# One block for the four stages behind the attention, with the loads of each inside the one in front

## The reference, cut to what matters

```python
x = x + tanh(g_xattn[0]) * cross_attention_16_heads(layernorm(x), ctx, mask)
x = x + tanh(g_ffn[0]) * expert_choice(layernorm(x))
#     softmax over 8 experts; each expert takes its 512 best tokens (top_k of the scores),
#     mid = silu(tokens @ W_up[group] + b_up); out = mid @ W_down[e] + b_down
#     y.at[idx].add(score * out): a token can be taken by several experts
x = x + tanh(g_xattn[1]) * bidirectional(layernorm(x), ctx)
#     Sim = e@w1 + q@w2 + (e*w3)@q.T + b;  hq = softmax(Sim) @ q;  hc = softmax(max(Sim)) @ e
#     concat[e, hq, e*hq, e*hc] @ W_qv + b_qv
x = x + tanh(g_ffn[1]) * first_choice(layernorm(x))
#     each token goes to its argmax expert while that has room for 512; gate * (x @ W[e].T + b[e])
```

## Time and profile before

| | |
|---|---|
| median of 3 runs | 819.12 us (817.71 to 821.33) |
| the profiled execution | 816.21 us |
| its span, first to last instruction | 814.5 us |
| PE / DVE / ACT / POOL busy | 654.6 / 435.8 / 317.2 / 276.8 us |
| mean granted TensorE clock | 0.907 of full speed |
| bytes moved | 99.96 MB, 123 GB/s |

### The profile page before, as it was taken

How to read it: one execution, slowest core, us unless ns; L and a number is a source line. 1 busy time by engine, 2 the same in 40 slices (tenths; PEclk the granted TensorE clock), 3 DMA queues, 4 the chain that set the end, 5 groups by cost and what they waited for, 6 DMA issues and landing times. The chain is left out here.

```text
span 814.5 us, 14651 instructions
## 1 busy us (share of the span) xinstructions
PE 654.6 (80%) x5225; PEld 452.9 (56%) x5225; DVE 435.8 (54%) x1306; ACT 317.2 (39%) x677; POOL 276.8 (34%) x386
## 2 busy tenths in 40 slices
PE   5999988999999850128999999953799999980783
PEld 3666545555555530023666666642688888860672
DVE  5646556777777637752111111102568887761683
ACT  2333335777777742223222222202655555310220
POOL 4101102344433411023555553332224444324275
PEclk9999999999999985557999999995899999996797
DMA  8579933666665119134363643227434341112772
GB/s 269 192 168 266 246 105 71 132 127 124 127 123 126 47 62 216 2 95 128 68 146 55 159 90 63 26 27 242 128 104 131 130 131 53 54 52 86 228 233 77
DMA packets 103343, 99.96 MB, mean 123 GB/s; under 512 B 21942, under 2 KB 95161, under 8 KB 103268
## 3 DMA queue, kind: packets, MB, share of 16 engines
q1 hardware_dynamic: 94056, 82.57, 39.4%
q0 software_dynamic: 9216, 16.46, 9.1%
HBM read 57.00 MB, written 42.25 MB: 122 GB/s over the span
## 5 line engine op out<-in xcount | busy, mean ns | idle before, releaser
L617 ACT ACTIVATE probs<-pb,b_key_cols 128x512 f32<-128x512 f32 x128 | 92.8, 780 | 16.7 <-PE pb L787 16.7
L484 DVE TENSOR_REDUCE neg_max<-pb 128x4 f32<-128x512 f32 x128 | 81.7, 680 | 3.0 <-PE pb L767 3.0
L1312 POOL DMA_INDIRECT scratch_resid<-y,s_idx x32 | 50.4, 1574 | 91.4 <-DVE y L1361 91.4
L1432 PE MATMUL pd<-w_dn,mid 128*128 128x256 f32 x320 | 73.3, 384 | 0.0
L1409 PE MATMUL pd<-gT,w_up 128*128 128x512 f32 x160 | 71.7, 604 | 0.9 <-DVE gT L1343 0.9
L1379 ACT ACTIVATE mid<-pd,b_up 128x512 f32<-128x512 f32 x40 | 27.4, 687 | 112.8 <-PE pd L1409 112.8
L1432 PEld LDWEIGHTS pd<-w_dn,mid 128*128 128x128 f32 x320 | 59.5, 190 | 12.7 <-issue 5.3
L1303 POOL DMA_INDIRECT rows<-scratch_rows,s_idx x32 | 31.3, 977 | 62.5 <-POOLq L49 50.0
L1361 DVE TENSOR_SCALAR y<-pd,gate 128x256 f32<-128x256 f32 x32 | 15.5, 484 | 68.7 <-PE pd L1432 61.9
L1409 PEld LDWEIGHTS pd<-gT,w_up 128*128 128x128 f32 x160 | 31.0, 194 | 37.1 <-issue 36.7
L365 POOL CAST nm_parts<-neg_max 128x16 bf16<-128x16 f32 x32 | 6.3, 198 | 123.4 <-DVE neg_max L484 123.4
(11 more groups left out here) (325 smaller groups left out, 1403.5 us busy)
## 6 DMA issues: line engine op xcount, KB each, us to landing
qs<-scratch_qparts SPq DMA_DIRECT2D x48, 128.0 KB, 4.5
ks<-scratch_kparts SPq DMA_DIRECT2D x48, 128.0 KB
w_dn<-in_W_down SPq DMA_DIRECT2D x8, 640.0 KB
scratch_slots<-s_zero SPq DMA_DIRECT2D x1, 4160.0 KB, 14.9
g_rows<-scratch_slots SPq DMA_DIRECT2D x8, 520.0 KB, 5.1
c_in<-in_ctx SPq DMA_DIRECT2D x8, 512.0 KB, 6.6
s_x<-in_x SPq DMA_DIRECT2D x8, 512.0 KB, 7.3
scratch_ctxT<-cT SPq DMA_DIRECT2D x8, 512.0 KB, 6.5
```

What stands on the lines that cost most here:

```text
L484: V.tensor_reduce(neg_max[:, h:h + 4], ps_s[b][:].rearrange("p (h k) -> p h k", h=4), AX.X, ALU.max, negate=True).then_inc(max_s, 1)
L617: A.activation(probs[2 * u + b][:], ps_st[b][:].rearrange("p (h q) -> p h q", h=4), ACT.Exp, bias=key_cols[:, 1, t:t + 1], scale=key_cols[ ...
L1312: pool.indirect_dma_start(out=T["resid"], out_offset=bass.IndirectOffsetOnAxis(ap=S["idx"][:, e, c:c + 1], axis=0), in_=y[e % 2][:, c, :], ...
L1432: ins = nc.tensor.matmul(here(c), mid[e % 2][m][:, c * P:(c + 1) * P], w_dn[e % 2][:, m, :], start=False, stop=(m == MT - 2))
```

## The change

The four stages behind front become four functions that return a Stage, a record of the instruction lists of each engine. behind_attention calls them and puts their lists one behind the other in a single nc.Block, with one set of semaphores and one set of eight PSUM banks. What must outlive a stage, or is loaded ahead of it, has a place of its own in SBUF (weights of both FFNs, W_qv, context tiles, tables); the rest of FFN, bidirectional stage and last stage shares places. d_rows becomes part of s_x1. Where the end of a Block held a stage back, a wait on a semaphore now does. Some semaphores of single waits in the routing are merged.

```diff
+        @block.sync
+        def _(sp):
+            route.on_sync(sp)
+            ffn.first_weights(sp)
+            bidir.small_loads(sp)
+            ffn.on_sync(sp, {4: route.clear_slots, 5: bidir.bulk_loads, 6: last.first_weights})
+            bidir.on_sync(sp)
+            last.on_sync(sp)
+        @block.gpsimd
+        def _(pool):
+            route.on_gpsimd(pool)
+            bidir.tables_on_gpsimd(pool)
+            ffn.on_gpsimd(pool)
+            bidir.on_gpsimd(pool)
+            last.on_gpsimd(pool)
...
+            route.on_vector(dve)
+            bidir.tables_on_vector(dve)
+            ffn.on_vector(dve)
...
+            route.on_tensor(pe)
+            bidir.tables_on_tensor(pe)
+            ffn.on_tensor(pe)
```

Routing and FFN:

```diff
-            sp.dma_start(T["slots"].rearrange("(t p) d -> p t d", p=P),
-                         S["zero"][:].unsqueeze(1).broadcast_to([P, TOKENS // P, ROW1])).then_inc(cleared_s, 16)
             sp.wait_ge(shift_s, 1)
...
-            sp.wait_ge(out_s, 32)
-            sp.wait_ge(cleared_s, 16)
+    def clear_slots(sp):
+        sp.dma_start(T["slots"].rearrange("(t p) d -> p t d", p=P),
+                     S["zero"][:].unsqueeze(1).broadcast_to([P, TOKENS // P, ROW1])).then_inc(cleared_s, 16)
...
-            V.tensor_tensor(S["idx"][:], tiles[:], inside[:], ALU.add)
+        V.tensor_tensor(S["idx"][:], tiles[:], inside[:], ALU.add).then_inc(idx_s, 1)
...
+    def first_weights(sp):
+        group(sp, 0)
+        expert(sp, 0)
+        group(sp, 1)
+        expert(sp, 1)
+    def on_sync(sp, behind):
+        for e in range(1, EXPERTS):
+            if e >= 2:
+                expert(sp, e)
+            if e % 2 and e // 2 + 2 < EXPERTS // 2:
+                group(sp, e // 2 + 2)
+            if e in behind:
+                behind[e](sp)
...
+        pool.wait_ge(route.idx_s, 1)
+        pool.wait_ge(route.rows_out, 32)
         gather(0)
         gather(1)
...
-            pool.wait_ge(added, EXPERTS * 16 * ST)
```

Bidirectional stage:

```diff
+    def bulk_loads(sp):
+        load_cT(sp, 0)
+        load_c(sp, 0)
+        sp.dma_start(w_f[:], T["W_qv"].rearrange("(b h p) n -> p b h n", p=P, h=HALVES)).then_inc(wf_s, 16)
+        load_cT(sp, 1)
+        load_c(sp, 1)
+        load_c(sp, 2)
+    def on_sync(sp):
+        sp.wait_ge(ffn.added, ffn.all_added)
+        for q in range(3):
+            load_x(sp, q)
...
-            sp.wait_ge(stored_s, 16 * QUADS)
...
             pool.wait_ge(dest_s, u + 1)
+            pool.wait_ge(route.cleared_s, 16)
...
-            pool.wait_ge(sent_s, 16 * TILES)
...
+    def tables_on_vector(dve):
+        dve.wait_ge(tab_s, 7)
...
+    def tables_on_tensor(pe):
+        pe.wait_ge(route.found_a, 16)
+        pe.wait_ge(tab_s, 7)
+        pe.wait_ge(w_s, 64)
+        for h in range(HALVES):
+            ins = M.matmul(ps_m[:, 0:E], ones[:], wg[:, h, :], start=(h == 0), stop=(h == HALVES - 1))
+        ins.then_inc(mid_ps, 1)
+        pe.wait_ge(mid_s, 3)
```

Last stage:

```diff
-                sp.dma_start(rows[e % 4][:], slots_t[:, bass.ds(e * ST, ST), :]).then_inc(in_s[e % 4], 16)
-                sp.dma_start(w[e % 4][:], T["W1"][bass.ds(e, 1)].rearrange("a (h p) n -> p (a h) n", p=P)).then_inc(w_in[e % 4], 16)
...
+    def weights(sp, e):
+        if e >= 4:
+            sp.wait_ge(y_s, (e - 3) * ST)
+        sp.dma_start(w[e % 4][:], T["W1"][e].rearrange("(h p) n -> p h n", p=P)).then_inc(w_in[e % 4], 16)
+        sp.dma_start(bias[e % 4][:], T["b1"][e].partition_broadcast(P)).then_inc(w_in[e % 4], 16)
+    def first_weights(sp):
+        for e in range(4):
+            weights(sp, e)
+    def on_sync(sp):
+        sp.wait_ge(bidir.sent_s, 16 * TILES)
+        for e in range(EXPERTS):
+            if e >= 4:
+                weights(sp, e)
+            sp.dma_start(rows[e % 4][:], slots_t[:, e * ST:(e + 1) * ST, :]).then_inc(in_s[e % 4], 16)
+    def on_gpsimd(pool):
+        pool.wait_ge(bidir.stored_s, 16 * QUADS)
```

More of the change, by code:

```diff
@@ L913, in route_top_k @@
[L913 to L942, removed]
-        ps = [ctx.enter_context(nc.psum_tensor(f"pc{i}", [P, 512], F32)) for i in range(8)]
@@ L955, in route_top_k, with keep @@
-        cleared_s, reach_s, sel_s = sem("pc_cleared"), sem("pc_reach"), sem("pc_sel")
-        moves_s, split_s, base_s, cnta_s, end_s, ways_s = (sem("pc_" + n) for n in ("moves", "split", "base", "cnta", "end", "ways"))
-        candidates = lambda i: i + 4 if i < HIGH else i + 7
-        shift_s, lg_s = (sem("pc_" + n) for n in ("shift", "lg"))
+        def keep(name, count, shape, dtype=F32):
+            S[name] = [ctx.enter_context(nc.sbuf_tensor(f"k_{name}{i}", shape, dtype)) for i in range(count)]
@@ L959, in route_top_k @@
+        with ExitStack() as part:
+            sb = lambda n, s, d=F32: part.enter_context(nc.sbuf_tensor(n, s, d))
+            last = first_choice_stage(nc, S, T, sem, sb, ps, bidir)
         block = ctx.enter_context(nc.Block())
@@ L1000, in _ @@
+            ffn.on_gpsimd(pool)
+            bidir.on_gpsimd(pool)
+            last.on_gpsimd(pool)
         @block.scalar
         def _(act):
-            act.wait_ge(sub_s, 1)
-            nc.scalar.activation(ex[:], ex[:], ACT.Exp).then_inc(ex_s, 1)
-            act.wait_ge(keyT_s, 1)
-            nc.scalar.activation(keys[:], ps_k[:, 0:2 * P], ACT.Copy).then_inc(key_s, 1)
-            act.wait_ge(split_s, 2)
[L1007 to L1012, removed]
-                with nc.allow_low_precision(reason="whole numbers up to 256 are exact"):
-                    nc.scalar.activation(junk_a[:], (high if i < HIGH else part)[:], ACT.Sign, bias=cand[i % 2][:, 3:4],
-                                         accum_out=count[i % 2][:, 2:3]).then_inc(cnta_s, 1)
@@ L1016, in _ @@
[L1016 to L1025 removed]
+            route.on_scalar(act)
@@ L1189, in _ @@
+            ffn.on_vector(dve)
+            bidir.on_vector(dve)
+            last.on_vector(dve)
         @block.tensor
         def _(pe):
[L1191 to L1202 removed]
@@ L1222, in _ @@
-            ins.then_inc(riseT_ps, 1)
-            pe.wait_ge(riseT_s, 1)
-            for g in range(2):
-                pe.wait_ge(step_s, g + 1)
-                for c in range(CAP // P):
-                    for e in range(4 * g, 4 * g + 4):
-                        rows = slice(e % 4 * TT, (e % 4 + 1) * TT)
-                        ins = nc.tensor.matmul(ps[e][:, c * P:(c + 1) * P], reach[rows, g, c * P:(c + 1) * P], riseT[rows, g, :],
-                                               start=True, stop=True)
-                ins.then_inc(look_ps, 4)
```

2216 lines of the change are left out of this document (1123 added, 1093 removed).

## The result

The changed kernel takes 807.12 us in the median of 4 runs (804.61 to 808.94); the kernel before, in the same comparison, 818.41 (815.94 to 821.33). The ratio is 0.987, with a 95% interval from 0.984 to 0.990. The forecast was 810.3 with a range of 800.5 to 815.0. The profiled execution took 807.32 with a span of 805.6, so 8.9 less than the 816.21 of before; the forecast for it was 8.8 less. Such closeness is partly luck: several terms were off and cancel, and routing begins at 306.4 instead of 305.1 in this execution, before anything that was changed. Counted from there the gain is 10.2 us.

The account below looks back on a forecast made before the run. PE's full plateaus bound the kernel, POOL the final experts; holes between stages hold drains of 83 ns per indirect DMA. Terms -5.3 - 0 - 6.2 - 5.3 + 8.0 = -8.8 take 819.1 to 810.3 us, range 800.5 to 815.0.

Parts of the forecast that it names:

- Part A: Routing to FFN: no Block end and early first weights let gathers land in 2.8 us; gain 5.3, bounds 1.5 to 5.6.
- Part B: Inside the FFN: clear, bulk loads and final-expert weights moved there cost 0, bounds 0 to 3 us.
- PE is full: FFN: PE works 21.91 of 22.00 us at full clock, so a gain below zero cost is excluded.
- Part C: FFN to bidirectional stage: x loads issued once all adds land, without the drain; gain 6.2 us, bounds 5.9 to 6.6.
- Part D: Bidirectional to last stage: earlier start 3.9, load order 1.9, late rows -0.5; gain 5.3 us, bounds 0.7 to 6.6.
- The chain to the first scatter: Last stage: closer row loads shorten rows of expert 0 to PE's first multiplication; gain 1.9 us, bounds 1.2 to 2.7.
- POOL, not DVE, sets the pace: Final experts: POOL bounds all but 3.0 of 41.9 us, so later rows cost only 0.5 us, bounds 0 to 4.4.
- Part E: Kernel end: one drain for 128 indirect DMAs takes 10.6 instead of 2.67 us; loss 8.0, bounds 0 to 10.
- three points lie on one line: Final drain: three earlier drains cost 83 ns per indirect DMA, carried on to 128 for the loss of 8.0 us.
- Rival 1: Final drain does not add up and stays near 2.7 us; total 802.3, chance 0.25.
- Rival 2: FFN and last-stage loads: prefetch was already hidden, gathers still slow, order gives nothing; total 815.9, chance 0.09.
- Rival 3: POOL's scatters: descriptor space runs out with 128 indirect DMAs in one Block; 42 us more, 852, chance 0.04.

Follow-up runs that it names:

- e2: Changed kernel with the first FFN weights issued only when the index tile is ready; 818.49 us, where the kernel before takes 828.90 on that chip.
- f3: Changed kernel with final experts' rows, weights and bias issued expert by expert, none inside the FFN (repeat of e3); 0.6 us below f1.
- g4: Kernel before with 136 unused semaphores allocated in its last stage; 818.92 us in one execution.
- f1: The changed kernel unaltered, run on a second chip as base for variants there; 806.06 us.
- e3: Changed kernel with final experts' rows, weights and bias issued expert by expert, none inside the FFN; 820.90 us, kernel before 828.90 on that chip.
- f2: Changed kernel with row loads of final experts 4 to 7 issued ahead of weights and bias; 1.3 us below f1, ranges overlapping.
- e4: Changed kernel with extra POOL drains after adds of experts 5 and 6 and in bidirectional steps; 811.77 us, kernel before 828.90 on that chip.
- f4: Changed kernel with rows first for experts 4 to 7 and POOL drains in pauses; 800.75 us, changed kernel 806.06 on that chip.
- g2: Changed kernel with rows first for experts 4 to 7 and one POOL drain at the final experts' start; 799.00 us, 0.978 of the kernel before.
- g3: Kernel of g2 plus throw-away PE transposes ahead of the FFN's and final experts' first turns; 797.35 us, 0.976 of the kernel before.
- e1: Separate kernel without the layers: Blocks of 16 to 192 indirect DMAs, each landed before its end; the drain of 128 took 6.79 us.
- g1: Separate kernel without the layers: Blocks of 100 to 256 gathers, plus narrow and 16-row gathers; the drain of 128 full gathers took 2.49 us.

## Why the prediction was right, and where only its sum was

**Part A** (forecast -5.3, measured -5.3): right with its reason. The gathers land in 2.8 us, and e2 takes 3.5 of the gain away by moving the weights alone.

**Part B** (0, measured +0.9): the loads cost nothing, as said. In the window of the earlier trace rows, where the clear begins, and in the next two, in which most of the loads come in, PE is as full as before:

```profile
430.00:452.00 22.00, 21.91 (x90) 13.99 (x89) 4.05 (x10) 4.97 (x8) 11.14 (x9) 1.00 0.61 141
447.00:470.00 23.00, 22.91 (x95) 14.88 (x94) 4.30 (x11) 4.97 (x8) 10.19 (x8) 1.00 1.07 322
470.00:490.00 20.00, 19.91 (x81) 12.23 (x80) 3.98 (x10) 4.97 (x8) 10.17 (x8) 1.00 1.09 329
```

The 0.9 arises before the first expert's y: from first up-projection to it 15.8 us before and 16.7 after; the rest is 155.4 in both. The step that put this at nothing, "PE is full", left out the clock. The windows from the first up-projection on, of the kernel before, then of the changed one:

```profile
372.12:375.50 3.38, 3.38 (x4) 1.48 (x5) 1.50 (x4) 0.00 (x0) 2.02 (x3) 0.50 0.35 98
375.50:381.00 5.50, 5.50 (x14) 2.47 (x13) 0.00 (x0) 3.29 (x5) 1.80 (x2) 1.00 0.27 74
```

```profile
368.17:373.60 5.43, 5.43 (x7) 2.33 (x8) 1.54 (x4) 1.58 (x2) 4.02 (x5) 0.51 0.38 103
373.60:379.00 5.40, 5.40 (x14) 2.33 (x13) 0.00 (x0) 2.45 (x4) 0.71 (x1) 1.00 0.19 50
```

Work that is full at both levels spends 5.43 instead of 3.38 us at 1.2 GHz; 2.05 us at half speed is 1.0 us lost. That is the whole of the 0.9. But it is not the work of the change, as the other kernels show:

```
                     first up-projection   granted clock in the
                     to last add           first 8 us of it
before, f3                 171.2                 0.79
before with g4's edit      171.3                 0.77
f1, the same again         171.4                 0.76
e3                         171.5                 0.76
e2, f2                     172.0                 0.69, 0.68
changed kernel             172.1                 0.67
e4, f4                     172.2                 0.66
g2                         172.3                 0.66
g3, work ahead             171.0                 0.81
```

The stage's length follows the clock, and the clock does not follow the wait. f1 is the changed kernel itself, and f3 has the same early up-projection and the clock of before; e2, where the wait is long again (12.7 us), has 0.69. So when the clock rises differs between executions, by some 2 us, and that is worth 1 us here. Whether the change makes the late rise more frequent, these single executions don't show.

**Part C** (-6.2, measured -6.2): right; the chain behind the x load kept its 13.1 us.

**Part D** (-5.3, measured -5.2): right in sum, wrong in two terms. The Block end gave 3.9 as forecast. The chain to the first scatter gave 4.4 instead of 1.9. (The working itself gives 1.2 to 1.8 up to PE's first multiplication: 11.5 less 9.8 to 10.3. The 1.9 lies just outside it.) Up to that multiplication it gave 3.2: the rows of expert 0 are scaled 3.7 us after their issue and not 4.4 to 5.0, and the two sets of turns take 3.15 us and not 3.9, since the clock rises in them. The rest, taken as unchanged, gave 1.2, since the multiplications of expert 0 ran nearly all at full clock (3.71 instead of 4.88 us; with f2's slower clock the gain of the chain is 2.9). The late rows cost 3.1 instead of 0.5, near the bound of 4.4. The step that failed is "POOL, not DVE, sets the pace": that held only while rows came in time. They were issued 1.2 us later, as forecast, and landed another 1 to 2.4 us later than that, and POOL waits 1.52 and 2.17 us for y. f2 shows that term, f3 both together.

**Part E** (+8.0, measured +5.4): the mechanism, 83 ns per DMA since the last drain, is shown by e1, g1, e4 and g2, with two exceptions in e1 (the Block of 112 and the last one, 1.1 and 1.3 us above the line). The step that failed is "three points lie on one line": they stood at 32, 32 and 64 DMAs and were carried to 128. With gathers of 128 rows the line breaks between 112 and 116 in g1 and between 96 and 128 in e1. The drain of 128 DMAs in the changed kernel is 7.16 and not 10.6, a loss of 4.5. The freeing of semaphores, taken at 0, is 0.9. Rival 1 (nothing adds up) is thus partly true: the counts add up, but beyond some number part of them is missing from the drain.

Rival 2 fell with e2. Rival 3 fell with g1: 256 in one Block were issued 1.25 us apart throughout.

So the mechanism was right, and the closeness of the number was luck in part. Within D, 2.5 us too little and 2.6 too much cancel; the 2.6 us by which E fell short of its forecast were then hidden in the profiled execution by the 0.9 of the FFN and by a front part that ended 1.3 us later. The medians differ by 11.3 us, not by 8.8.

## What to carry to other kernels

Look at what the end of a Block costs on POOL's queue before merging Blocks: merging does not remove the drain but moves it to the last place, where nothing hides it. A drain of one's own, put where POOL waits for others, removes it (g2: 4.5 us at the end for one line). When loads are brought forward, keep the order in which consumers need them, data before weights in a queue whose issues take 0.4 us each and whose first entry waits. And a term of the sum is only as good as the clock in its window: before a loss of 1 us is put down to a change, the same kernel's granted clock in a second execution should be looked at.

## What the hardware showed beyond that

- A GpSimd DRAIN behind indirect DMAs that have all landed costs 82 to 85 ns for each since the last drain, independent of rows, bytes and kind, up to 96 of them (e1) or 112 (g1). For gathers of 128 rows 98 are missing from 116 on (g1), and 46 from 128 on in e1; one drain of e1 took 1.3 us more than its count.
- Clearing and freeing 136 semaphores more takes 0.9 us.
- TensorE's clock can rise and fall again within 10 us at a stage's start (0.84, 0.50, 0.98 in g3), and the 16 multiplications of one expert ran at either level in two executions that begin the stage alike (3.71 and 4.89 us). In the same kernel the FFN's first 8 us had a granted clock of 0.67 in one execution and of 0.76 in another.
